# Leaving out two runs of repeated TensorE products in a graph and LSTM kernel

## The reference

```
h = relu(adj @ (x @ Wg0 + bg0)); h = relu(adj @ (h @ Wg1 + bg1))
for p in 1..4:                      # LSTM over windows of p nodes
    h[:, p-1::p] = last hidden state of the LSTM with weights p over each window
x = layernorm(x + h)
agg = A_hat @ x                     # A_hat: adj + I, scaled by degrees
h = relu(batchnorm(agg @ W1.T + b1))        # 256 channels
out = batchnorm(h @ W2.T + b2)              # 128 channels
x = layernorm(x + out)
```

## Time and profile before

| | us |
|---|---|
| median of three runs | 801.25 |
| the profiled execution's own time | 800.9 |
| its span | 799.1 |
| TensorE busy in it | 776.7 (97%) |
| VectorE busy | 714.0 (89%) |
| ScalarE busy | 598.1 (75%) |
| GpSimd busy | 107.8 (13%) |

### The profile page before, as it was taken

How to read it: one execution, slowest core, us unless ns; L and a number is a source line. 1 busy time by engine, 2 the same in 40 slices (tenths; PEclk the granted TensorE clock), 3 DMA queues, 4 the chain that set the end, 5 groups by cost and what they waited for, 6 DMA issues and landing times.

```text
span 799.1 us, 15542 instructions
## 1 busy us (share of the span) xinstructions
PE 776.7 (97%) x4964; PEld 533.3 (67%) x4964; DVE 714.0 (89%) x1818; ACT 598.1 (75%) x1190; POOL 107.8 (13%) x118
## 2 busy tenths in 40 slices
PE   8999999999999999999999999999999989999985
PEld 6666777777767777777777777767776656444542
DVE  4787989999999999999999999989999998788996
ACT  4777777777777777777787778686868765797598
POOL 0000000000000000000000000000000101187695
PEclk9999999999999999999999999999999999999999
DMA  5110001010101010101010101010000000155245
GB/s 202 31 49 1 1 27 55 27 53 28 53 28 54 26 52 26 52 26 52 26 52 26 52 26 52 27 53 28 27 27 28 27 27 27 53 174 169 88 177 210
DMA packets 17694, 44.45 MB, mean 56 GB/s; under 512 B 2032, under 2 KB 3184, under 8 KB 17520
## 3 DMA queue, kind: packets, MB, share of 16 engines
q1 hardware_dynamic: 17504, 43.81, 15.3%
q10 hardware_dynamic: 144, 0.07, 0.0%
HBM read 27.09 MB, written 16.78 MB: 55 GB/s over the span
## 4 chain that ended last, share of the span: by engine, by line
PE 81%; DVE 9%; ACT 5%; issue 2%; DMA 1%; SPq 1%; POOL 0%; ACTq 0%; DVEq 0%; POOLq 0%
PE gate_bank L969 15%; PE gate_bank L970 14%; PE gate_bank L984 6%; PE gate_bank L994 6%; PE gate_bank L1047 5%; PE back_bank L923 3%; PE front_bank L879 3%; ACT z L1202 3%; PE front_bank L896 3%; PE front_bank L884 3%; PE front_bank L890 3%; PE gate_bank L953 3%; PE gate_bank L954 3%; PE gate_bank L955 3%; PE gate_bank L977 3%
## 5 line engine op out<-in xcount | busy, mean ns | idle before, releaser
L969 PE MATMUL gate_bank<-h_hi,w_hi 128*128 128x256 f16 (+2 forms) x528 | 162.3, 307 | 4.3 <-DVE h_lo L1418 2.9
L970 PE MATMUL gate_bank<-h_hi,w_lo 128*128 128x256 f16 (+2 forms) x528 | 162.2, 307 | 0.0
L1135 ACT ACTIVATE gate_i<-gate_bank,lstm_bias 128x512 f32<-128x512 f32 (+2 forms) x176 | 99.6, 566 | 62.1 <-PE gate_bank L994 32.6
L1135 ACT ACTIVATE gate_o<-gate_bank,lstm_bias 128x512 f32<-128x512 f32 (+2 forms) x176 | 100.0, 568 | 31.0 <-PE gate_bank L994 20.9
L984 PE MATMUL gate_bank<-h_lo,w_hi 128*128 128x256 f16 (+2 forms) x384 | 116.2, 303 | 0.0
L969 PE MATMUL gate_bank<-s_hi,w_hi 128*128 128x256 f16 (+2 forms) x384 | 113.0, 302 | 0.5 <-DVE s_hi L1415 0.4
L970 PE MATMUL gate_bank<-s_hi,w_lo 128*128 128x256 f16 (+2 forms) x384 | 113.0, 302 | 0.0
L1401 DVE SCALAR_TENSOR_TENSOR gate_f<-gate_o,gate_f 128x512 f32<-128x512 f32 (+2 forms) x176 | 94.7, 538 | 19.8 <-ACT gate_f L1141 18.7
L766 POOL TENSOR_TENSOR rstd<-veps,neg_half 128x8 f32<-128x8 f32 x15 | 26.3, 1750 | 627.4 <-DVE veps L1341 627.4
L1141 ACT ACTIVATE gate_f<-cell 128x512 f32<-128x512 f32 (+2 forms) x176 | 89.7, 510 | 28.1 <-DVE cell L1398 14.7
L1135 ACT ACTIVATE gate_g<-gate_bank,lstm_bias 128x512 f32<-128x512 f32 (+2 forms) x176 | 99.5, 565 | 0.6
(11 more groups left out here) (263 smaller groups left out, 1722.8 us busy)
## 6 DMA issues: line engine op xcount, KB each, us to landing
x_kept<-normed_sb SPq DMA_DIRECT2D x16, 512.0 KB, 2.6
z<-x_kept SPq DMA_DIRECT2D x16, 512.0 KB, 3.7
rows_sb<-in_x SPq DMA_DIRECT2D x15, 512.0 KB, 3.3
x_front<-in_x SPq DMA_DIRECT2D x15, 512.0 KB, 4.2
out<-z SPq DMA_DIRECT2D x15, 512.0 KB, 3.1
z<-in_wr SPq DMA_DIRECT2D x1, 1536.0 KB, 6.7
x_front<-in_x SPq DMA_DIRECT2D x2, 256.0 KB, 3.4
out<-z SPq DMA_DIRECT2D x2, 256.0 KB, 2.6
```

The lines of the kernel that those rows point to most:

```text
L969: mm(dst, w[0], v[0], start=start, stop=False)
L970: mm(dst, w[1], v[0], start=False, stop=False)
L1135: ins = activation(acts[gate][h][:, 0:n], gate_bank[h][bank_of(job, gate)][:, 0:n], ACT.Tanh if gate == "g" else ACT.Sigmoid, bias=lstm_bi ...
```

## The change

The two calls with 18 products are left out, and with them the names that only they used. The 8 products at the program's start stay. Nothing takes their place: TensorE stands at its next wait, for `last_normed` and for `w2_ready`.

```diff
-        warm_bank = gate_bank[0][2]
...
-        STAY_WARM = 18
         WARM_UP = 8
...
             wait(pe, ("back", "z_stats", 3), GROUPS - 1, 0)
-            keep_warm(warm_bank, STAY_WARM)
             for n in range(2):
                 pe.wait_ge(last_normed[n], 1)
...
                 mm(last_z_bank(n)[:], gw1_hi[:, n % 2, :], low, start=False, stop=True).then_inc(last_z, 1)
 
-            keep_warm(warm_bank, STAY_WARM)
 
             pe.wait_ge(w2_ready, 3)
```

## The result

The changed kernel takes 804.1 us (median of 7 runs, 802.95 to 806.02) against 801.31 us (7 runs, 801.15 to 801.59) of the kernel before: ratio 1.0034, 95% interval [1.0023, 1.0046]. It is slower by 2.8 us; 803.5 was forecast. A second measurement beside another set of runs of the kernel before gave 804.47 against 801.21, ratio 1.0039 [1.0025, 1.0052]. One execution was profiled: 803.25 us, span 801.5, 2.4 us more than before. The code lines behind the deleted ones have moved: L1016 is now L1013, L1047 is L1043, L1504 is L1500.

The account below looks back on a forecast made before the run. TensorE was taken to bound the 50 us from 690.3, while both runs fill its idle time. Gap costs 1.2 + 1.1 less 0.05 gave 2.25 us; from the median, 803.5 us, 8-in-10 range 801.4 to 805.4.

Parts of the forecast that it names:

- Part 2: TensorE, where the runs stood: idle gaps of 4.4 and 4.0 us appear and bring the granted clock down.
- the price of 1.7 us: One clock fall in dense TensorE work: half of a 3.40 us stretch at 0.50 is lost, 1.7 us.
- Part 1: Both runs: 36 products leave, worth at most 0.11 us in the second run, nothing in the first; 0.05 taken.
- First gap: TensorE idle from 676.55 to 681.01; a fall there slows the work up to 686.3; 1.2 us taken.
- the case given as the most: First gap: clock low from 681.01 to 686.3, costing about 2.6 us.
- the least: First gap: a late fall partly taken by 0.8 us of slack, 0.9 us; or no fall, 0.
- Second gap: TensorE idle from about 686.26 to 690.29; a fall costs L1047's stage up to 1.7 us or more; 1.1 taken.
- the forecast's own bracket: Whole kernel: both gaps cost something, 1.6 to 3.4 us, giving 802.9 to 804.7 us; chance 0.55.
- rival B: Both gaps: both falls in full or a long low time, 804.7 to 805.5 us; chance 0.13.
- the 803.15 worked out for it: Whole kernel, profiled execution: 800.9 us before plus the forecast loss of 2.25 us.
- The stage behind: L1047's stage, 50 us from 690.3: TensorE has no slack, so time lost at its start is lost at the end.
- What was to be seen: Profile after: clock at 0.50 between 677 and 696, L1047 0 to 2 us later, its stage's last product 1.6 to 3.4 later.

Follow-up runs that it names:

- the longer second run: Against the kernel before: first run kept at 18 repeated products, second raised from 18 to 26; 802.86 us, ratio 1.0021.
- the kernel with twelve products: Against the kernel before: both runs of repeated products kept, but with 12 products each instead of 18; 801.95 us, ratio 1.0008.
- the first series: Kernels without one run, with 12 and with 26 products, measured beside the kernel before on the same chip; kernel before's median 801.22 us.

## Why the prediction was right

**The direction and its mechanism.** Part 2 named a fall of the clock behind each gap as the price, against a chain of waits that promised 3.9 us of gain. Both falls are in the profile after, and each of them comes back alone when only its run is left out. The trace had the case in small: 2.89 us of idle time and then 0.50. But the price of 1.7 us, half of that row's 3.40, is not what that fall itself cost: there it was 0.4 to 0.7 us. It is the price in work that TensorE bounds, and the second gap paid it.

**Part 1 (at most 0.11 us, 0.05 taken).** Right: without the second run L1046 starts 9.28 us behind L1016, exactly as with it. The gain is nothing, and the 0.11 us were an artefact of modelled ends.

**First gap (1.2 us).** The step held: 1.1 us in the profiled execution, 1.3 in that of the second measurement. In the kernel without the first run it was more, 1.7 in the profile and 1.64 by the medians. There the low stretch began before L1015 and lasted to 686.7. That was the case given as the most, and its price of 2.6 us was too high: the 0.8 us of slack was taken off the least and not off the most. With it, 1.8 us, near the 1.7 measured.

**Second gap (1.1 us, two thirds of 1.7).** This term was mis-sized: 1.46 us in the profiled execution, 1.64 by the medians of the kernel without the second run. I had let part of the low time fall into the gap, or be shared with the first; in the profiled execution 0.5 of the 3.4 us did fall into the gap, in that of the kernel without the second run nothing did. The full 1.7 us was nearer.

**The sum.** 2.25 forecast, 2.8 and 3.3 us measured. 804.1 lies in the forecast's own bracket of 802.9 to 804.7, 804.47 near its end and not far from rival B. Two of the seven executions, at 805.92 and 806.02, lie above the range. That the profiled execution, 803.25, came within 0.1 us of the 803.15 worked out for it is partly luck: it lost 2.57 us in the two gaps and had no fall at 655 us, where the kernel before's execution had one.

**The stage behind.** "What it loses at their start is lost at the end" was argued from busy shares; the longer second run showed it: L1047 1.70 us later, ScalarE's first instruction behind the stage 1.62 us later.

**What was to be seen** was seen: ScalarE's L1169 at 679.1 and L1013 at 680.8, released by it, against 679.5 and 681.0; 0.50 in two stretches; L1043 0.86 us later. TensorE's last product of that stage is 2.3 us later.

## What to carry to other kernels

A product whose result nobody reads can still do work: before deleting one, look at the idle time that opens in its place and at what the granted clock did behind idle times of that length elsewhere in the trace. The chain of waits shows where time passes, not what would be saved; ask what the next instruction waited for (here the weights, at 690.20, against a run that ended at 690.14). And price a fall of the clock in the stage where its low time lies: in one that TensorE bounds, half of it is lost at the end (1.70 us of 3.4 here); where TensorE waits for other engines anyway, less (0.4 to 0.7 us of 3.4, behind the wait at 655 us).

## What the runs showed of the hardware

Falls behind the same wait differ between executions: behind the 2.89 us at 655 us there was none in three profiled executions (the changed kernel's first, the one without the second run, the longer second run), 3.4 us at the low level in the kernel before's and three more, and 6.8 us in that of the kernel with twelve products. The kernel before also has a spread that its first seven runs (0.44 us) did not show: its 35 runs of the first series lie between 800.26 and 803.43 us. That these falls make all of that spread was not shown. A wait of only 1.91 us, early in the program, also had a low stretch behind it, from 18.4 to 21.8 us, and so had the same wait of 1.87 us in the first kernel with the wait at 655 us filled, from 17.6 to 21.0. What decides between a fall and none was not worked out here.
